# Storing expert results beside their input rows with SyncE, and fetching them token by token with GpSimd at the end

## What is computed

```python
x = x + conv_attention(layernorm_over_channels(x))     # per image, 256 positions
t = tokens(x)                                          # [2048, 64]
flat = layernorm(t)
probs = softmax(flat @ router_w.T)                     # 8 experts
topk_probs, topk_idx = top_k(probs, 2)                 # weights scaled to sum 1
h = silu(flat @ w1[e].T) * (flat @ w3[e].T)            # 682 hidden channels
y = h @ w2[e].T
out = t + sum over the token's 2 experts of gate * y
```

## Time and profile before

| what | value |
|---|---|
| median of 3 runs | 176.17 us (174.99 to 176.45) |
| span of the profiled execution, first to last instruction | 238.2 us |
| mean granted TensorE clock in it | 0.799 of full |
| busy: TensorE matmul, VectorE, ScalarE, GpSimd | 166.9, 99.7, 70.8, 85.7 us |
| GpSimd's 39 result scatters, 32 row scatters | 37.4 us, 31.6 us |

### The profile page before, as it was taken

One profiled execution on the slowest core, in us unless ns is written; L12 is line 12 of the kernel. 1 busy time (PEld: TensorE's weight loads), 2 busy tenths in 40 slices (PEclk: granted clock), 3 DMA queues, 4 the chain that ended last, 5 costly groups with the idle time before them and its releaser, 6 DMA issues.

```text
span 238.2 us, 4880 instructions
## 1 busy us (share of the span) xinstructions
PE 166.9 (70%) x1682; PEld 139.1 (58%) x1682; DVE 99.7 (42%) x372; ACT 70.8 (30%) x141; POOL 85.7 (36%) x114
## 2 busy tenths in 40 slices
PE   3595957428683069589494994958949697895683
PEld 2364836307452068588393983948839597783543
DVE  2557568255583037584222433223232344342230
ACT  2377433013310034224232142222422323333101
POOL 2963577723277700603205033060230604142400
PEclk9999586555578559979799598895997979798579
DMA  6990000184570229652958075390661600000053
GB/s 185 322 297 20 11 25 22 31 267 151 159 290 23 50 81 328 216 210 46 364 169 313 3 240 196 88 346 4 203 228 42 266 10 14 11 15 11 17 176 91
DMA packets 19893, 33.00 MB, mean 139 GB/s; under 512 B 7691, under 2 KB 13100, under 8 KB 19868
## 3 DMA queue, kind: packets, MB, share of 16 engines
q1 hardware_dynamic: 16732, 29.55, 37.8%
q0 software_dynamic: 2272, 2.35, 3.0%
q10 hardware_dynamic: 864, 0.79, 1.0%
HBM read 25.55 MB, written 7.13 MB: 137 GB/s over the span
## 4 chain that ended last, share of the span: by engine, by line
issue 48%; POOL 21%; PE 11%; DVE 8%; DMA 3%; another core or an unknown queue 3%; ACT 3%; POOLq 1%; SPq 0%; ACTq 0%; DVEq 0%
POOL ys L370 15%; POOL xs L361 5%; PE psum L925 3%; PE psum L914 2%; ACT xn L426 2%; DMA y_in<-ys 2%; DVE rows L595 1%; PE psum L894 1%; PE psum L1103 1%; PE psum L885 1%; DMA ys<-y_out,y_row 1%; DMA proj<-projections 1%; DVE index L606 1%; DVE neg_max L584 1%
## 5 line engine op out<-in xcount | busy, mean ns | idle before, releaser
L370 POOL DMA_INDIRECT ys<-y_out,y_row x39 | 37.4, 960 | 104.0 <-DVE y_out L839 95.2
L827 DVE TENSOR_TENSOR hid<-psum,act_sb 128x512 f32<-128x512 f32 (+1 forms) x50 | 33.4, 676 | 88.9 <-ACT act_sb L504 61.6
L1031 PE MATMUL psum<-x_cols,weights 64*128 64x128 f32 x390 | 52.9, 286 | 13.9 <-issue 12.1
L1031 PEld LDWEIGHTS psum<-x_cols,weights 64*128 64x128 f32 x390 | 47.6, 193 | 19.4 <-issue 15.8
L1033 PE MATMUL psum<-x_cols,weights 64*128 64x128 f32 x390 | 53.1, 286 | 0.9 <-issue 0.9
L504 ACT ACTIVATE act_sb<-psum 128x512 f32<-128x512 f32 (+1 forms) x50 | 28.7, 586 | 70.0 <-remote 42.4
L1033 PEld LDWEIGHTS psum<-x_cols,weights 64*128 64x128 f32 x390 | 47.7, 193 | 1.1 <-issue 1.1
L1059 PE MATMUL psum<-hid,weights 128*64 128x128 f32 x468 | 42.8, 357 | 2.1 <-issue 1.1
L1059 PEld LDWEIGHTS psum<-hid,weights 128*64 128x64 f32 x468 | 39.3, 189 | 4.8 <-issue 2.7
L361 POOL DMA_INDIRECT xs<-xrows,pos x32 | 31.6, 987 | 12.9 <-issue 8.9
L1037 PE MATMUL psum<-x_cols,weights 64*106 64x128 f32 x78 | 8.7, 349 | 23.1 <-ACT act_sb L504 18.4
(11 more groups left out here) (148 smaller groups left out, 189.9 us busy)
## 6 DMA issues: line engine op xcount, KB each, us to landing
weights<-experts SPq DMA_DIRECT2D x39, 565.0 KB
xs<-zeros SPq DMA_DIRECT2D x4, 1040.0 KB, 11.1
x_in<-xs SPq DMA_DIRECT2D x39, 32.5 KB
ys<-y_out,y_row POOLq DMA_INDIRECT x39
xs<-xrows,pos POOLq DMA_INDIRECT x32
y_in<-ys ACTq DMA_DIRECT2D x2, 256.0 KB, 4.5
y_in<-ys SPq DMA_DIRECT2D x2, 256.0 KB, 4.3
x_sb<-x_tok SPq DMA_DIRECT2D x1, 384.0 KB, 3.4
```

The lines of the kernel that those rows point to most:

```text
L370: nc.gpsimd.indirect_dma_start(ys, bass.IndirectOffsetOnAxis(ap=y_row[:, j:j + 1], axis=0), y_out[:, i % RING, h, :], None).then_inc(y_sca ...
L827: nc.vector.tensor_tensor(live(i, hid[:, i % 2, s, :]), live(i, H3_BANK[g % 3]), live(i, act_sb[:, g % 3, :]), ALU.mult).then_inc(hid_done, 1)
L1031: first_ = nc.tensor.matmul(H1_BANK[g % 2][:, src], weights[0:C, slot, P * s:P * (s + 1)], x_cols[0:C, i % 2, src], start=True, stop=True)
```

## The change

`ys` gets the shape of `xs`: 2048 rows for each expert. A slot's results are stored to the rows from which its inputs came, by SyncE, with plain DMAs at the table's row (`store_results`). The stores of quad i-4 stand in SyncE's queue between the row loads and the weight loads of quad i, and those of the last four quads behind the loop. The row is read again from the table for each of them. Like `xs`, `ys` is filled with zeros at the start, by four more DMAs of SyncE.

At the end GpSimd waits until all stores have landed, and fetches both results of every token to `y_in` by `pos`: 32 indirect DMAs of 128 rows each (`gather_results`). VectorE waits for the eight gathers of a quarter. Row numbers, `keep`, `occupancy` and `y_row` are gone, rows have 64 words instead of 65, and a normalised token is written once to `xrows` and scattered from there twice.

```diff
-RW = C + 1
-ID = C
-PARK = K_TOP * CAP
-YROWS = PARK + NS * SUB
-        xrows = sb("xrows", [P, TILES, K_TOP, RW])
+        xrows = sb("xrows", [P, TILES, C])
...
-        def load_results(engine, q):
-            by_token = ys[0:PARK, :].rearrange("(p t k) c -> p t k c", t=TILES, k=K_TOP)
-            engine.dma_start(y_in[:, quarter(q), :, :], by_token[:, quarter(q), :, :]).then_inc(y_loaded[q], 16)
...
             for q in range(QUARTERS):
-                part = xs[E * CAP // QUARTERS * q:E * CAP // QUARTERS * (q + 1), :]
-                sp.dma_start(part.rearrange("(p r) c -> p (r c)", p=P).rearrange("p (r z) -> p r z", z=ZW),
-                             zeros[:].unsqueeze(1).to_broadcast([P, 8, ZW])).then_inc(xs_cleared, 16)
+                clear(xs, q, xs_cleared)
+            for q in range(QUARTERS):
+                clear(ys, q, ys_cleared)
...
+            def store_results(i):
+                at = rows_of(i)
+                if i == 0:
+                    sp.wait_ge(ys_cleared, 16 * QUARTERS)
+                sp.wait_ge(y_out_ready, i + 1)
+                for h in members(i):
+                    sp.dma_start(ys[bass.ds(at[h], SUB), :], y_out[:, i % RING, h, :]).then_inc(y_stored[i % RING], 16)
...
                     load_rows(i, at)
+                    if i >= QUAD:
+                        store_results(i - QUAD)
                     load_weights(i, owners_of(i))
-
-            all_scattered(sp)
-            for q in range(0, QUARTERS, 2):
-                load_results(sp, q)
+            for i in range(NQ - QUAD, NQ):
+                store_results(i)
...
-            def scatter_result(j):
-                i, h = divmod(j, QUAD)
-                if h == 0:
-                    pool.wait_ge(y_out_ready, i + 1)
-                    pool.wait_ge(y_row_ready, i + 1)
+            def gather_results(t, k):
+                p, at = t // TPP, t % TPP * K_TOP + k
                 nc.gpsimd.indirect_dma_start(
-                    ys, bass.IndirectOffsetOnAxis(ap=y_row[:, j:j + 1], axis=0),
-                    y_out[:, i % RING, h, :], None).then_inc(y_scattered[i % RING], 16)
+                    y_in[:, t, k, :], None, ys,
+                    bass.IndirectOffsetOnAxis(ap=pos[:, p, at:at + 1], axis=0)
+                    ).then_inc(y_gathered[t // (TILES // QUARTERS)], 16)
...
-            for j in range(NS):
-                scatter_result(j)
+            all_stored(pool)
+            for t in range(TILES):
+                for k in range(K_TOP):
+                    gather_results(t, k)
...
-                dve.wait_ge(y_loaded[q], 16)
+                dve.wait_ge(y_gathered[q], 16 * K_TOP * TILES // QUARTERS)
```

More of the change, by code:

```diff
@@ L58 @@
 RING = 4
-ZW = E * CAP * RW // (QUARTERS * P * 8)
+ZW = E * CAP * C // (QUARTERS * P * 8)
 def metaformer(nc, x_tok, projections, value_output, experts, xs, ys, out):
@@ L83, in metaformer @@
         slot_at = sb("slot_at", [P, NS])
-        slot_no = sb("slot_no", [P, 1])
         zeros = sb("zeros", [P, ZW])
-        y_row = sb("y_row", [P, NS], I32)
         weights = sb("weights", [P, WSLOTS, WW])
@@ L148, in metaformer @@
         row_at = sb("row_at", [P, NS])
-        limit = sb("limit", [P, NS])
         table = sb("table", [P, 2, NS], I32)
-        keep = sb("keep", [P, NS], I32)
-        x_in = sb("x_in", [P, XRING, QUAD, RW])
+        x_in = sb("x_in", [P, XRING, QUAD, C])
         x_pairs = sb("x_pairs", [P, 2, QUAD, 2, C])
@@ L175, in metaformer @@
         ones_made, tables_made = sem("ones_made"), sem("tables_made")
-        zeros_made, xs_cleared = sem("zeros_made"), sem("xs_cleared")
+        zeros_made, xs_cleared, ys_cleared = sem("zeros_made"), sem("xs_cleared"), sem("ys_cleared")
         dve_step = sem("dve_step")
@@ L194, in metaformer @@
         shifted, exponents, gates_ready = sem("shifted"), sem("exponents"), sem("gates_ready")
-        keep_ready, table_ready = sem("keep_ready"), sem("table_ready")
+        table_ready = sem("table_ready")
         w_loaded = [sem(f"w_loaded{i}") for i in range(WSLOTS)]
         x_in_loaded = [sem(f"x_in_loaded{i}") for i in range(XRING)]
-        x_paired, y_row_ready, hid_cleared = sem("x_paired"), sem("y_row_ready"), sem("hid_cleared")
+        x_paired, hid_cleared = sem("x_paired"), sem("hid_cleared")
         x_turned, x_cols_ready = sem("x_turned"), sem("x_cols_ready")
@@ L203, in metaformer @@
         y_copied, y_turned, y_out_ready = sem("y_copied"), sem("y_turned"), sem("y_out_ready")
-        y_scattered = [sem(f"y_scattered{i}") for i in range(RING)]
-        y_loaded = [sem(f"y_loaded{q}") for q in range(QUARTERS)]
+        y_stored = [sem(f"y_stored{i}") for i in range(RING)]
+        y_gathered = [sem(f"y_gathered{q}") for q in range(QUARTERS)]
         y_weighted = sem("y_weighted")
@@ L214, in metaformer @@
         TAIL_BANKS = psum[:, 1:3, 0:2 * SUB]
-        TABLES = 9 + PHASES
+        TABLES = 6 + PHASES
         CONST_DMAS = 2
@@ L246, in images, with all_stored @@
             return slice(B // QUARTERS * q, B // QUARTERS * (q + 1))
-        def all_scattered(engine):
+        def all_stored(engine):
             for r in range(RING):
-                engine.wait_ge(y_scattered[r], 16 * sum(len(members(i)) for i in range(r, NQ, RING)))
-        def load_results(engine, q):
-            by_token = ys[0:PARK, :].rearrange("(p t k) c -> p t k c", t=TILES, k=K_TOP)
-            engine.dma_start(y_in[:, quarter(q), :, :], by_token[:, quarter(q), :, :]).then_inc(y_loaded[q], 16)
+                engine.wait_ge(y_stored[r], 16 * sum(len(members(i)) for i in range(r, NQ, RING)))
         def store(engine, q, h):
@@ L264, in _, with clear @@
         def _(sp):
+            def clear(where, q, cleared):
+                part = where[E * CAP // QUARTERS * q:E * CAP // QUARTERS * (q + 1), :]
+                sp.dma_start(part.rearrange("(p r) c -> p (r c)", p=P).rearrange("p (r z) -> p r z", z=ZW),
+                             zeros[:].unsqueeze(1).to_broadcast([P, 8, ZW])).then_inc(cleared, 16)
             early = (slice(0, TPP), slice(TPP, TILES))
@@ L362, in scatter_row @@
                     xs, bass.IndirectOffsetOnAxis(ap=pos[:, p, at:at + 1], axis=0),
-                    xrows[:, TPP * p + at // K_TOP, at % K_TOP, :], None).then_inc(dispatched[phase_of(p)], 16)
-            def scatter_result(j):
-                i, h = divmod(j, QUAD)
-                if h == 0:
-                    pool.wait_ge(y_out_ready, i + 1)
-                    pool.wait_ge(y_row_ready, i + 1)
+                    xrows[:, TPP * p + at // K_TOP, :], None).then_inc(dispatched[phase_of(p)], 16)
+            def gather_results(t, k):
+                p, at = t // TPP, t % TPP * K_TOP + k
                 nc.gpsimd.indirect_dma_start(
-                    ys, bass.IndirectOffsetOnAxis(ap=y_row[:, j:j + 1], axis=0),
-                    y_out[:, i % RING, h, :], None).then_inc(y_scattered[i % RING], 16)
+                    y_in[:, t, k, :], None, ys,
+                    bass.IndirectOffsetOnAxis(ap=pos[:, p, at:at + 1], axis=0)
+                    ).then_inc(y_gathered[t // (TILES // QUARTERS)], 16)
             nc.gpsimd.memset(ident[:], 0.0).then_inc(ident_zeroed, 1)
@@ L396, in _ @@
                 count_up(slot_at[:, OPENED[p]:OPENED[p + 1]], [[SUB, OPENED[p + 1] - OPENED[p]]], 0, 0)
-            count_up(slot_no[:], [[1, 1]], 0, 1)
-            count_up(y_row[:], [[SUB, NS]], PARK, 1)
             nc.gpsimd.affine_select(out=upto[:], in_=upto[:], compare_op=ALU.is_ge, fill=0.0, base=0,
@@ L533, in _ @@
             nc.scalar.activation(expo[:], shift[:], ACT.Exp).then_inc(exponents, 1)
-            all_scattered(act)
-            for q in range(1, QUARTERS, 2):
-                load_results(act, q)
             for q in range(QUARTERS):
@@ L632, in normalise_t @@
                 for t in range(TPP * p, TPP * (p + 1)):
-                    ins = nc.vector.tensor_scalar(xrows[:, t, :, 0:C], rows[:, t:t + 1, E:TX].to_broadcast([P, K_TOP, C]),
+                    ins = nc.vector.tensor_scalar(xrows[:, t, :], rows[:, t, E:TX],
                                                   moments_t[:, t, 0:1], rstd_t[:, t:t + 1], ALU.subtract, ALU.mult)
@@ L714, in used_up @@
                 chain(nc.vector.tensor_tensor(used[:, p, 1:], used[:, p, 1:], given[:, before_], ALU.subtract))
[L716 to L727, removed]
             def gate_shifts():
@@ L780, in pair_up @@
                     dve.wait_ge(x_turned, i - 1)
-                nc.vector.tensor_copy(x_pairs[:, i % 2, 0:n, :, :], x_in[:, slot, 0:n, 0:C].unsqueeze(2)
+                nc.vector.tensor_copy(x_pairs[:, i % 2, 0:n, :, :], x_in[:, slot, 0:n, :].unsqueeze(2)
                                       .to_broadcast([P, n, 2, C])).then_inc(x_paired, 1)
[L783 to L789, removed]
             for p in range(PAIRS):
@@ L836, in results @@
                 if i >= RING:
```

(10 more changed lines are left out.)

3 lines of the change are left out of this document (removed).

## The result

The changed kernel takes 235.03 us (median of 4 runs, 234.57 to 235.81), against 175.58 us before (median of 4 runs, one more than the 176.17 at the start stands for). The ratio is 1.338, with a 95% interval of 1.330 to 1.346. That is 59.4 us longer, where 35.1 had been forecast, and lies above the range of 201 to 221 us.

What follows compares the result with a forecast made beforehand. No engine was busy throughout; the end, from last result copy to last instruction, was taken to decide. 33.6 (end) + 0.5 (clock) + 1.5 (SyncE) - 0.5 (small edits) = +35.1 us on 176.17: 211.3 us, range 201 to 221.

Steps and rivals of the forecast that it cites:

- the term for SyncE in the quads: Quads 4 to 9: SyncE's turn of 12.9 us against quads of 10.9, mostly covered; +1.5 us, bounds 0 to 6.
- The end: After the last result copy: stores land, 32 gathers at 1.265 us, last quarter exposed; +33.6 us, plus 0.5 for the clock.
- a quicker: Second rival, gathers at the end: GpSimd is faster unprofiled, pace 0.96 us, total 202 us; chance 0.13.
- a dearer: Third rival, gathers at the end: a gather costs more than a scatter, pace 1.53 us, total 219.5 us; chance 0.12.
- a not overlapping gather: Fourth rival, at the end: each gather starts only when the one before has landed, +28.7 us, total 240; chance 0.03.
- not slower: Fifth rival, at the end: unprofiled gathers so cheap that the end costs no more than now, 176 us; chance 0.02.
- the length of a timed quad: Quads: nine in 125.7 us, less 28 us of nameless waits, gives 97.7 us, or 10.9 us each.
- the cover: Quads: three weight buffers let SyncE run two quads ahead; less transfer and late start, about 11 us of lead.
- The first rival: Quads: SyncE becomes the bound, 12.9 against 10.9 us, 6 in place of 1.5, total 216 us; chance 0.22.
- The small edits: VectorE's dropped or narrowed instructions, -0.5 us, bounds -2 and 0; zeros of `ys` at the start, 0, at worst +2.
- its two extremes: Whole kernel: low 198.3 us with gathers at a pace of 0.96, high 227.0 us if everything goes badly.
- The base: Whole kernel: most of the profile's 62 us excess is disturbance in the quads, so the difference is added to 176.17 unscaled.

Runs made afterwards that it cites:

- the second profile: The kernel of before, profiled again with no edit: 176.2 us against 175.3 for the same kernel beside it, ratio 1.005, with a span of 173.6 us.

## Why the prediction was wrong

The direction, the mechanism at the end and its size were right. The step that failed is the term for SyncE in the quads, forecast as +1.5 us, bounds 0 to 6, and measured as +25.2. It accounts for 23.7 of the 24.3 us by which the time was missed. The prediction named the sign of it, VectorE or TensorE waiting for `x_in` or `weights`, and a stage of the quads that moves by more than 6 us, and both came. Point by point:

**The end.** Forecast +34.1 (33.6 and 0.5 for the clock), measured +35.5, and 35.9 by taking the gathers out. The steps: first gather 3.9 us after the end of the last copy, measured 184.39 - 180.27 = 4.1; pace 1.265, measured 1.25 for most and 1.28 on average, since two gathers took 1.46 in place of 0.94 us; landing 2.2, measured 2.5 (226.66 - 224.17). ("13 in a row keep it" was read too kindly: of the twelve steps between those 13 scatters two are 1.33 and 1.35 us.) The granted clock was at 1.2 GHz for the last quarter (5 tenths in the page's row), after 8.5 us in which TensorE stood idle, and its eight entries took 2.08 us. With matmuls kept going ahead of them the granted clock was 1.00 and they took 1.16. So the clock cost 0.9 us: the 0.5 taken for it was too little, the bound of 1.0 was right. The rivals of a quicker, a dearer and a not overlapping gather all fell, and so did "not slower".

The Trainium skill, page "DMA: Bandwidth & Descriptors", section "Anatomy of one DMA — SWDGE (gpsimd) path", gives a DMA issued by GpSimd a fixed cost of about 2.0 us. This profile agrees with it as the time to landing (2.4 us), and not as a price for each: 32 of them took 42.3 us with the last landing, not over 64.

**SyncE's turn.** The length was right: forecast 12.9 us, measured 13.7. What failed is what it was set against: how long a quad is, and how far SyncE is ahead. Two steps went wrong.

First, the length of a timed quad. I had subtracted the waits of the earlier trace rows for nameless releasers from the disturbed profile and got 10.9 us for a quad. It is 9.0 us. The disturbed execution had lost time in ways that those rows don't name: from 90 to 215 us its TensorE had a mean granted clock of 0.86 and was busy for 99.2 of 125 us, where the second profile shows 1.00 and no pause in its 51 us:

```profile
90.00:215.00 125.00, 99.19 (x1273) 90.16 (x1270) 48.66 (x107) 38.35 (x70) 33.59 (x35) 0.86 0.45 156
```

What disturbed it is not on record. The shortfall of a turn was therefore not 2 us but 13.7 - 9.0 = 4.7, or 28 us in six turns.

Second, the cover. I counted the three weight buffers as a lead of two quads, some 11 us. A buffer is only a lead if the queue that fills it is ahead, and SyncE wasn't: its turn of 9.2 us was as long as a quad, it never waited for a free buffer in the second profile, and rows came about 1 us late for VectorE already. In the kernel of before with four more entries a turn, 13 to 14 us of added reads cost 12.6 us (10 to 14 by the interval of the ratio), and in the change a shortfall of 28 us cost 25.2. So the cover was a few us at most, and not 11. The disturbed profile had hidden that, since there TensorE was the slow one, and SyncE stood 22.2 us waiting for it to free weight buffers, a wait that the second profile doesn't have at all:

```profile
SPq L281 <- PE psum L1059: 22.2, 5, 5.9
```

The first rival, "SyncE becomes the bound of the quads", was the right mechanism, with a chance of 0.22. But it was priced with the same two numbers, at 216 us, so that the range missed the time even with it.

**The small edits.** Forecast -0.5. The front is between 61.7 and 64.3 us in the profiles of kernels with and without the change, so nothing of this size can be told. The zeros of `ys` took 11.5 us to issue (four DMAs) in place of the 6.9 that was forecast, and cost nothing that shows: the front of the changed kernel is not longer. Their effect alone wasn't tried.

**The sum.** The bounds of 1.5 and 4 us for the landing of the last stores were left out of its two extremes. With them these are 197.4 and 228.6 us, and 235 lies outside all the same.

**The base.** I took the 62 us between profile and median as disturbance, to be left out. That was right, and the second profile shows it. What was wrong was to go on and read the balance of two engines from the disturbed stage.

## What to carry to other kernels

Price an instruction on a queue that feeds the bounding engine against that engine's clean time for a step. If the two are equal, nearly every addition is paid: here 24 reads of a table entry cost 12.6 us, and the same reads and stores cost nothing in the quads on a queue with nothing to do (93.3 us against 92.9). When a profile's span is far from the timed runs, durations of single instructions and the pace of an undisturbed queue carried over here, but which engine leads in a stage did not. And turning scatters that are hidden, one piece at a time, into gathers that need all the results moved their whole cost to the end, 35 us.

## What the runs showed of the hardware that was not expected

One kernel gave one profile of 238.2 us and one of 173.6 us, with the same number of instructions, while its timed runs all lay between 173.7 and 180.4 us. In the long one GpSimd's pace was the same to 0.01 us, 1.26 to 1.27 from one result scatter to the next in both.

GpSimd issues a plain DMA of 128 rows much faster than an indirect one: four stores in 2.31 us, 0.58 each, against 1.25 us from one gather to the next.

```profile
123.20 2.31 POOL L360 DMA_DIRECT2D ys<-y_out  x4 [6.66 <-DVE y_out L815]
```

A few gathers take longer than the rest, and not at random. In the four kernels with gathers, seven take 1.39 to 1.46 in place of 0.94 us, and each of them starts 0.04 to 0.12 us after VectorE has begun to weight a quarter:

```profile
216.11 0.69 DVE L841 TENSOR_TENSOR weighted<-y_in,gates 128x512 f32<-128x512 f32 x1 [9.81 <-DMA y_in<-ys,pos]
216.15 1.46 POOL L367 DMA_INDIRECT y_in<-ys,pos  x1 [0.30 <-issue]
```

Five others start within 0.04 us of such an instruction on either side and keep their 0.94 to 0.95 us, and there VectorE's instruction takes 0.70 to 0.76 us in place of 0.69. So these two instructions seem to hold each other up, a gather by half a microsecond and VectorE's by less than 0.1. Why they do is not shown.
